# Sixteen sequences through two gated layers on one Trainium2 core: the output gate's products taken out of the first norm's loop, the routing of layer 0 put ahead of the first chunk's gates, and each group's stores issued as two pairs

## The chip, the core and the metric

The kernel runs on one core of a Trainium2 chip. The core has TensorE (PE, matrix products, with its weight loads shown as PEld), VectorE (DVE), ScalarE (ACT), GpSimd (POOL) and SyncE (SP, used here for DMA queues only). The engines run side by side and wait for each other by semaphores. The metric is the device time of one execution in microseconds (us), a median over runs.

## The reference: what is computed

Tokens `x` (16 sequences of 256 tokens of 128 values, 4096 tokens) go through two layers, and each is `x + s * silu(f)`. In layer 0, `s` is a gated linear attention in chunks, and `f` a mixture of 8 experts of which each token uses two; in layer 1, `s` is causal attention with 16 heads and `f` a mixture of 16 experts, again two for each token.

```python
xn = _layernorm(x, axis=-1)
# attention of layer 0: q, k, v, decays gk from a low-rank product, in chunks of 64
gk = jax.nn.log_sigmoid(x @ Wgk1 @ Wgk2 + bgk2) / GATE_NORM
o = _gla_chunk(q, k, v, gk)
g = (x @ Wg).reshape(B, T, H, DV)
o = o * jax.lax.rsqrt(jnp.mean(o * o, axis=-1, keepdims=True) + EPS) * gnw
o = o * (g * jax.nn.sigmoid(g))
s = o.reshape(B, T, H * DV) @ Wo
# experts of layer 0
gate_scores = jax.nn.softmax(jnp.einsum('btd,ed->bte', x, Wg), axis=-1)
topk_val, topk_idx = jax.lax.top_k(gate_scores, TOP_K)
...
x = x + s * g
```

`g * sigmoid(g)` of the attention is the output gate that the change moves; its products are `xn @ Wg`.

## The kernel before, in words

All engines follow one walk, a fixed order of steps written in `walk`; each engine's block gives its own body for a step. The order on an engine is therefore the order of the walk, and a wait holds back everything behind it on that engine.

**First norm (0 to about 44 us).** `norm(0, g)` runs over 8 groups of 512 tokens, in stages that lag behind each other: DVE centres and takes variances, ACT scales, PE turns the rows (L385), DVE moves them to `xnT` (L1228), PE makes the routing logits (L368), DVE moves those (L1246) and chooses two experts for each token (`choose`, L1270 to L1286). Behind each group's logits PE makes the output gate's product of that group (L374, 128x512 f32, eight in all) and ACT applies Silu (L831).

**First gates and routing (44 to about 60 us).** `gla(-1)` and `gla(0)` make the low-rank gate product (`gate_in` L419), its rest (`gate_out` L431), the gate logarithms on ACT (`gate_logs` L891 to L895) and the sigmoids on DVE (L1372). Then `route(0)`: PE counts tokens of each expert (L405), ACT moves the counts (L855), and DVE works out the slot of each row of each token (L1304 to L1318), then the experts of each group and the mixing weights (L1323 to L1344).

**Scatter (60 to about 155 us).** POOL writes the 8192 token rows to their slots in HBM (`xs`) with 64 indirect DMAs (L1718), spread over the walk's `gla(1)` to `gla(6)`. Two of a chunk's steps are POOL's too: `chunk_ends` (L1748), which waits for the exponentials of the decays (ACT L904, behind DVE's scan L1380), and `output_gates` (L1754), which waits for `o_rs` of ACT L941. DVE's `set_later` (L1189 to L1201) prepares constants; it stands in the walk behind the first scatter step of `t=1`.

**Experts of layer 0 with the attention (155 to about 414 us).** 18 groups of 512 rows. For group `g`, SP loads its rows, PE turns them (L558), makes the products with the expert's weights in two halves of two experts (`expert_up`, L594 to L598) and, a group later, the product down (L608); DVE adds the bias (L1477); POOL stores four blocks of 128 rows by indirect DMA (`store`, L1734, 4 for a group). Until `t=19` chunk steps of the attention stand between them: on PE `key_values` (L482), `outputs` (L496, L503) and others, on DVE the scan L1380, `states` (L1400 to L1408) and `gated` (L1431). Four PSUM banks go round among all these products, so a product can wait for an older one's bank; the bank of `key_values` is free when DVE L1406 has read it.

**Join, second norm, routing, scatter, experts of layer 1 (414 to 970 us).** The same machinery, with 20 groups and with the attention's heads between them (`mha`). In a group's loop POOL multiplies tanh by sine (`product1`, L1774), copies the slots' ids (L1727), adds phases (L1769) and stores (L1734). Then a last join to the end at 1017.6 us.

## Time and profile before

| | |
|---|---|
| Time, median of 3 runs | 1022.38 us (1019.39 to 1028.81) |
| Time of the profiled execution | 1020.89 us |
| Its span (first to last instruction) | 1017.6 us |
| PE busy | 758.3 us (75%) |
| DVE busy | 641.5 us (63%) |
| ACT busy | 633.3 us (62%) |
| POOL busy | 468.1 us (46%) |

The profile is of one execution. A busy share is an average over stages with different limits, so each stage is read by itself: which engine has no gaps there, and what its first instruction waited for. PE runs at one of two clock levels, 1.2 or 2.4 GHz; the column PEclk is the granted share of full speed.

### The profile page before, as it was taken

Reading aid. Unit: us, or ns where it says so; the run is one execution under the profiler, and the core shown is the slowest. Engines: PE = TensorE matmul, PEld = TensorE weight load, DVE = VectorE, ACT = ScalarE, POOL = GpSimd, SP = SyncE. Lnnn points to the kernel's source line nnn. Section 1 sums busy time; section 2 is a strip of 40 time slices with the busy share of each in tenths; the row PEclk is TensorE's granted clock in tenths of the full one; section 3 lists DMA queues with packets and bytes.
Section 4 is the critical chain, followed back from the end, with each engine's and each line's share of the span. In section 5 each row is a group of like instructions: output and inputs, shape, how many; then the busy total and the mean of one; then the engine's idle time right before and its main releaser. Section 6 shows DMA issues by size and latency. Waiting matters only on the chain.

```text
span 1017.6 us, 23699 instructions
## 1 busy us (share of the span) xinstructions
PE 758.3 (75%) x8916; PEld 600.5 (59%) x8916; DVE 641.5 (63%) x1113; ACT 633.3 (62%) x1151; POOL 468.1 (46%) x477
## 2 busy tenths in 40 slices
PE   4738678999999989057692788678878878878650
PEld 3427567888888988035471455456756756666530
DVE  7587555767676433597767676366467567566537
ACT  5437455777766532257461455566979878888756
POOL 4137882324242355542000777313656556556622
PEclk9659778999999999577796798689999999999985
DMA  9702211011111111700000533200111111111053
GB/s 312 281 23 69 73 58 51 23 33 33 34 30 36 43 54 46 194 11 1 1 2 0 193 94 114 61 12 25 41 33 38 39 33 41 35 34 30 22 154 107
DMA packets 62366, 63.92 MB, mean 63 GB/s; under 512 B 7378, under 2 KB 52322, under 8 KB 62132
## 3 DMA queue, kind: packets, MB, share of 16 engines
q1 hardware_dynamic: 53300, 43.99, 14.9%
q0 software_dynamic: 8960, 18.43, 5.5%
q8 instruction: 77, 1.26, 0.5%
q14 instruction: 29, 0.24, 0.1%
HBM read 31.84 MB, written 30.55 MB: 61 GB/s over the span
## 4 chain that ended last, share of the span: by engine, by line
PE 41%; DVE 20%; POOL 13%; issue 13%; ACT 9%; DMA 2%; SPq 0%; POOLq 0%; DVEq 0%; ACTq 0%
POOL xs L1718 8%; PE bank L594 4%; POOL ys L1734 4%; PE bank L442 3%; PE bank L596 3%; DVE arena L1592 3%; PE bank L657 3%; PE bank L595 2%; PE bank L722 2%; PE bank L608 2%; PE bank L482 2%; PE bank L622 2%; ACT L805 2%; ACT arena L1115 2%; DVE arena L1530 2%
## 5 line engine op out<-in xcount | busy, mean ns | idle before, releaser
L1734 POOL DMA_INDIRECT ys<-arena x152 | 171.6, 1129 | 182.7 <-DVE arena L1477 75.3
L1718 POOL DMA_INDIRECT xs<-arena x128 | 131.6, 1028 | 61.8 <-issue 33.9
L594 PE MATMUL bank<-arena 128*128 128x128 bf16 x608 | 138.9, 235 | 11.7 <-DVE arena L1592 6.5
L596 PE MATMUL bank<-arena 128*128 128x128 bf16 x608 | 138.6, 235 | 0.0
L595 PE MATMUL bank<-arena 128*128 128x128 bf16 x608 | 136.2, 231 | 0.0
L1115 ACT ACTIVATE arena<-bank 128x512 f32<-128x512 f32 x192 | 99.0, 605 | 54.2 <-PE bank L710 54.2
L1592 DVE TENSOR_REDUCE arena<-bank 128x2 bf16<-128x512 f32 (+1 forms) x192 | 118.9, 683 | 14.0 <-PE bank L683 14.0
L805 ACT ACT_TABLE_LOAD x72 | 92.4, 1283 | 1.3
L442 PE MATMUL bank<-arena 128*128 128x256 f32 x256 | 69.3, 431 | 15.4 <-DVE arena L1364 15.4
L594 PEld LDWEIGHTS bank<-arena 128*128 x608 | 63.5, 104 | 28.2 <-issue 18.8
L1505 DVE TENSOR_SCALAR arena<-bank 128x512 f32<-128x512 f32 x40 | 27.6, 691 | 74.5 <-ACT arena L1012 74.5
L1580 DVE SCALAR_TENSOR_TENSOR arena<-arena,bank 128x512 bf16<-128x512 bf16 x64 | 46.0, 745 | 44.2 <-ACT arena L1088 42.9
L442 PEld LDWEIGHTS bank<-arena 128*128 128x128 f32 x256 | 54.7, 220 | 25.2 <-DVE arena L1364 16.1
L1774 POOL TENSOR_TENSOR arena<-arena 128x1024 f32<-128x1024 f32 x19 | 44.6, 2348 | 49.5 <-ACT arena L1026 49.4
L596 PEld LDWEIGHTS bank<-arena 128*128 x608 | 62.6, 103 | 5.4 <-issue 1.0
L598 PE MATMUL bank<-arena 128*128 x288 | 64.5, 224 | 0.1
L657 PE MATMUL bank<-arena 128*128 128x256 f32 x256 | 63.6, 393 | 0.7 <-issue 0.7
L595 PEld LDWEIGHTS bank<-arena 128*128 x608 | 63.7, 105 | 0.2
L1467 DVE SCALAR_TENSOR_TENSOR arena<-arena,bank 128x512 f32<-128x512 f32 x36 | 24.6, 689 | 44.7 <-ACT arena L988 44.7
L657 PEld LDWEIGHTS bank<-arena 128*128 128x128 f32 x256 | 47.6, 196 | 8.3 <-issue 2.5
L988 ACT ACTIVATE arena<-bank 128x512 f32<-128x512 f32 x36 | 21.5, 598 | 45.7 <-PE bank L598 45.6
L1680 POOL TENSOR_TENSOR arena<-arena 128x4 f32<-128x4 f32 x16 | 16.2, 1013 | 72.5 <-DVE arena L1211 72.5
(214 smaller groups left out, 1971.6 us busy)
## 6 DMA issues: line engine op xcount, KB each, us to landing
xs<-arena SPq DMA_DIRECT2D x19, 516.0 KB, 8.1
arena<-xs SPq DMA_DIRECT2D x38, 258.0 KB, 2.8
arena<-ys SPq DMA_DIRECT2D x32, 256.0 KB, 5.3
arena<-in_MF SPq DMA_DIRECT2D x8, 512.0 KB, 4.2
ys<-arena POOLq DMA_INDIRECT x152, 2.3
arena<-in_x SPq DMA_DIRECT2D x8, 256.0 KB, 5.5
arena<-in_W SPq DMA_DIRECT2D x8, 256.0 KB
xs<-arena POOLq DMA_INDIRECT x128, 2.4
```

What stands on the lines that cost most here:

```text
L442: i = mm(k[:, 256 * h:256 * h + 256], (Wq, Wk)[n // 2][:, 128 * hh:128 * hh + 128], xnT[:, cols])
L594: mm(o, hi, b[:, 0, c4], stop=False)
L595: mm(o, hi, b[:, 1, c4], start=False, stop=False)
L596: i = mm(o, lo, b[:, 0, c4], start=False, stop=(l == 1))
L598: i = mm(o, b1r[:, 128 * c:128 * c + 128], b1s[:, bass.DynSlice(v * 128, 128)], start=False)
L657: j = mm(k[:, 256 * z:256 * z + 256], Wqk[:, c:c + 128], xnT[:, 256 * b:256 * b + 256])
L805: eng.preload_act_table_set(name)
L1115: act(PT[kt_][:, i, gs[0]:gs[0] + len(gs), :], bank_of["s2", b, n, i][:, :].rearrange("p (g q) -> p g q", q=w), ACT.Exp, scale=8 ** -0.5). ...
L1580: stt(T, hiT[n % 2], low_of[n // 2], bank_of["qk1", b, n][:, :], ALU.mult, ALU.add).then_inc(m_qk_moved.sem, 1)
L1592: red(negM[b % 2][:, u, 32 * i + gs[0]:32 * i + gs[0] + len(gs)], kv_, op=ALU.max, negate=True).then_inc(m_max.sem, 1)
L1718: eng.indirect_dma_start(xs[l][:, :], bass.IndirectOffsetOnAxis(ap=slot_i[l][:, m:m + 1], axis=0), xrow[:, t, :], None).then_inc(rows_move ...
L1734: eng.indirect_dma_start(ys[l][:, :], bass.IndirectOffsetOnAxis(ap=yid[g % 4][:, j:j + 1], axis=0), y[:, 128 * j:128 * j + 128], None).the ...
```

## The change

The walk's step `route` is cut in two, `route` and `route_end`; the products of the output gate become a step `silus` of their own; `store` takes a pair of blocks at a time.

```diff
             for g in range(NG + 5):
                 do["norm"](0, g)
                 if g == 4:
                     do["set_gates"]()
-            for t in range(-1, 1):
-                for part in range(3):
-                    do["gla"](t, part)
+            for part in range(3):
+                do["gla"](-1, part)
+            do["silus"](0, 2)
             do["route"](0)
+            do["silus"](2, NG)
+            for part in range(3):
+                do["gla"](0, part)
             for t in range(1, 7):
                 for part in range(3):
                     do["scatter"](0, 3 * (t - 1) + part, 18)
...
                 for c in range(8 * (t - 1) // 6, 8 * t // 6):
                     do["w1"](c)
+                if t == 1:
+                    do["route_end"](0)
...
             do["route"](1)
+            do["route_end"](1)
...
-                    if l == 0:
-                        b = bank(("silu", h), silu_done.at(h))
-                        if h == 0:
-                            eng.wait_ge(*ld["wvg"].at(0))
-                        mm(b[:, :], Wvg[:, 128:256], xnT[:, 512 * h:512 * h + 512]).then_inc(silu.sem, 1)
+
+            def silus(a, e):
+                for h in range(a, e):
+                    b = bank(("silu", h), silu_done.at(h))
+                    if h == 0:
+                        eng.wait_ge(*ld["wvg"].at(0))
+                    mm(b[:, :], Wvg[:, 128:256], xnT[:, 512 * h:512 * h + 512]).then_inc(silu.sem, 1)
...
-                h = due(l, CHOOSE, g)
-                if h is not None and l == 0:
-                    table(TANH_SIN)
+
+            def silus(a, e):
+                table(TANH_SIN)
+                for h in range(a, e):
                     eng.wait_ge(*silu.at(h))
                     act(s_all[:, 4 * h:4 * h + 4, :].rearrange("p t d -> p (t d)"), bank_of["silu", h][:, :], ACT.Silu).then_inc(silu_done.sem, 1)
...
+            def route_end(l):
                 if l == 0:
                     spread(0)
                     spread(1)
...
                 step(red(R["sl"], inc.rearrange("p (e b) -> p b e", e=E), op=ALU.add), 13)
                 step(cp(slot_i[l], R["sl"]), 14)
-                ef = R["ef"]
+
+            def route_end(l):
+                E, R, C = EXPERTS[l], RS[l], routed[l]
+                cu, en, ef, step = R["cu"], R["en"], R["ef"], step_of(C)
...
-            def store(l, g):
+            def store(l, g, pair):
                 y = (yb0, yb1)[l][g % 2]
-                eng.wait_ge(*y_out[l].at(g))
-                eng.wait_ge(*ids_moved[l].at(g))
-                for j in range(4):
+                if pair == 0:
+                    eng.wait_ge(*y_out[l].at(g))
+                    eng.wait_ge(*ids_moved[l].at(g))
+                for j in (2 * pair, 2 * pair + 1):
...
             def experts0(g, part):
+                if part == 0 and g >= 2:
+                    t = OUTPUTS_EARLY + g
+                    eng.wait_ge(*(kv.at(t - 3) if t < 19 else up[0].at(g, 1) if g < 18 else down[0].at(17)))
+                    store(0, g - 2, 1)
                 if part == 0 and g + 1 < GROUPS[0]:
                     ids(0, g + 1)
                 if part == 2 and g >= 1:
-                    store(0, g - 1)
+                    store(0, g - 1, 0)
+                    if g == 18:
+                        store(0, 17, 1)
...
             def experts1(g, part):
+                if part == 0 and 2 <= g < 20:
+                    eng.wait_ge(*up[1].at(g, 1))
+                    store(1, g - 2, 1)
                 if part == 0 and 1 <= g < 20:
                     product1(g - 1)
...
                 if part == 2 and g >= 1:
-                    store(1, g - 1)
+                    store(1, g - 1, 0)
+                    if g >= 19:
+                        store(1, g - 1, 1)
```

Below, PE's order from the end of the norm's loop to the second chunk's gates. L385 turns rows, L368 makes logits, L374 the output gate's product, L419 and L431 the chunk gates (`gate_in`, `gate_out`), L405 the counts. Before:

```order
L385 MATMUL bank<-arena 128x128 x4
L368 MATMUL bank<-arena 128x8 x4
L374 MATMUL bank<-arena 128x512
L368 MATMUL bank<-arena 128x8 x4
L374 MATMUL bank<-arena 128x512
L419 MATMUL bank<-arena 80x256
L431 MATMUL bank<-arena 128x256 x4
L419 MATMUL bank<-arena 80x256
L405 MATMUL bank<-arena 128x256 x4
L431 MATMUL bank<-arena 128x256 x4
```

The same place after the change, where line numbers are those of the changed file (L393 turns rows, L374 makes logits, L382 the output gate's product, L429 and L441 the chunk gates, L413 the counts):

```order
L393 MATMUL bank<-arena 128x128 x4
L374 MATMUL bank<-arena 128x8 x8
L429 MATMUL bank<-arena 80x256
L382 MATMUL bank<-arena 128x512 x2
L413 MATMUL bank<-arena 128x256 x4
L382 MATMUL bank<-arena 128x512 x6
L441 MATMUL bank<-arena 128x256 x4
L429 MATMUL bank<-arena 80x256
L441 MATMUL bank<-arena 128x256 x4
```

The counts now come ahead of the first `gate_out`, and six of the eight products of the output gate stand between the counts and it.

DVE's order behind the cast of the slots (L1335 in the changed file). L1384 and L1392 are the chunk gates, L1202 to L1214 are `set_later`, L1400 is the scan, L1441 and L1443 scale queries and keys, L1373 a part of the expert weights, and L1343 opens `route_end`, of which three rows are shown:

```order
L1335 CAST arena<-arena 128x64 [waits routed0]
L1384 TENSOR_TENSOR arena<-bank,arena 16x256 [waits gate1_hi,routed0]
L1392 SCALAR_TENSOR_TENSOR arena<-bank,arena 128x512 [waits gate2_ln]
L1392 SCALAR_TENSOR_TENSOR arena<-bank,arena 128x512
L1202 CAST arena<-arena 128x128 x3
...
L1400 SCALAR_TENSOR_TENSOR arena<-arena 128x1024 [waits decay,set_pool]
...
L1373 TENSOR_TENSOR arena<-arena 128x512 [waits w1_hi]
L1343 TENSOR_TENSOR arena<-arena 128x320
...
L1357 TENSOR_REDUCE arena<-arena 128x32 [waits chosen_exp,routed_exp,routed0]
...
L1364 TENSOR_TENSOR arena<-arena 128x32 [waits routed0]
L1400 SCALAR_TENSOR_TENSOR arena<-arena 128x1024 [waits decay,routed0]
```

Before, the two sigmoid rows stood ahead of the whole routing, and all of the routing ahead of `set_later` and the first scan; now the rest of the routing stands between the first and the second scan.

POOL's order in a loop of the experts of layer 0, before (L1754 `output_gates`, L1727 ids, L1748 `chunk_ends`, L1734 stores):

```order
L1754 TENSOR_TENSOR arena<-arena 128x256 [waits o_rs]
L1727 COPY arena<-arena 128x4 [waits ld_rows0,stored_y0]
L1748 COPY arena<-arena 128x12 [waits state,exp_decay]
L1734 DMA ys<-arena 9216x128 [waits ids_moved0,y_out0]
L1734 DMA ys<-arena 9216x128 x3
```

and after the change (L1781, L1747, L1775 and L1755 in the same roles):

```order
L1781 TENSOR_TENSOR arena<-arena 128x256 [waits o_rs]
L1755 DMA ys<-arena 9216x128 [waits kv]
L1755 DMA ys<-arena 9216x128
L1747 COPY arena<-arena 128x4 [waits ld_rows0,stored_y0]
L1775 COPY arena<-arena 128x12 [waits state,exp_decay]
L1755 DMA ys<-arena 9216x128 [waits ids_moved0,y_out0]
L1755 DMA ys<-arena 9216x128
```

Two of the four stores that stood ahead of the next loop's `output_gates` now stand behind it.

## Rows read from the trace of the kernel before

**Rows 1.** POOL's timeline, the scatter: start, duration, what, [idle before, releaser]

```profile
59.91 1.28 POOL L1718 DMA_INDIRECT xs<-arena  x1 [12.43 <-DVE arena L1318]
...
67.93 0.95 POOL L1718 DMA_INDIRECT xs<-arena  x1 [0.30 <-issue]
72.66 0.20 POOL L1748 COPY arena<-arena 128x12 f32<-128x12 f32 x1 [3.77 <-ACT arena L904]
...
86.23 0.20 POOL L1748 COPY arena<-arena 128x12 f32<-128x12 f32 x1
...
154.25 0.97 POOL L1718 DMA_INDIRECT xs<-arena  x1 [0.30 <-issue]
```

**Rows 2.** Windows, experts and attention of layer 0: stretch, length, busy of each engine

```profile
180.00:344.00 164.00, 160.99 (x2192) 143.08 (x2193) 112.17 (x186) 117.66 (x190) 57.60 (x65) 1.00 0.12 33
```

**Rows 3.** PE's timeline, products of the output gate (L374) and logits

```profile
24.46 1.10 PE L374 MATMUL bank<-arena 128*128 128x512 f32 x2
...
38.27 2.06 PE L374 MATMUL bank<-arena 128*128 128x512 f32 x2
40.12 1.71 PE L368 MATMUL bank<-arena 128*128 128x8 f32 x8
```

**Rows 4.** DVE's timeline from the last logits to the second scan

```profile
41.87 0.19 DVE L1246 COPY arena<-bank 128x32 f32<-128x32 f32 x1 [3.22 <-PE bank L368]
...
46.74 0.42 DVE L1364 TENSOR_TENSOR arena<-bank,arena 16x256 bf16<-16x256 f32 x1
...
53.09 1.22 DVE L1304 TENSOR_TENSOR_SCAN arena<-arena 128x512 f32<-128x512 f32 x1
...
59.41 0.20 DVE L1318 CAST arena<-arena 128x64 int32<-128x64 f32 x1
...
64.98 0.50 DVE L1189 CAST arena<-arena 128x128 bf16<-128x128 f32 x3
...
69.22 2.28 DVE L1380 TENSOR_TENSOR_SCAN arena<-arena 128x1024 f32<-128x1024 bf16 x1
...
79.33 2.33 DVE L1380 TENSOR_TENSOR_SCAN arena<-arena 128x1024 f32<-128x1024 bf16 x1
```

**Rows 5.** ACT's timeline, the table load, the gate logarithms and the counts

```profile
45.02 1.28 ACT L805 ACT_TABLE_LOAD   x1
47.87 1.09 ACT L891 ACTIVATE arena<-bank 128x512 f32<-128x512 f32 x2 [1.56 <-PE bank L431]
...
51.30 1.43 ACT L855 ACTIVATE arena<-bank 128x256 f32<-128x256 f32 x4
```

**Rows 6.** Windows of 2 us: PEclk stands behind the busy times

```profile
58.00:60.00 2.00, 0.96 (x3) 0.23 (x1) 1.90 (x4) 0.00 (x0) 0.09 (x1) 0.73 0.00 0
```

**Rows 7.** Timeline of all engines, a loop in the middle of layer 0's experts

```profile
249.84 2.27 POOL L1734 DMA_INDIRECT ys<-arena  x1 [0.30 <-issue]
...
252.12 0.91 DVE L1404 TENSOR_TENSOR arena<-arena 128x128 f32<-128x128 f32 x1
252.14 0.73 POOL L1754 TENSOR_TENSOR arena<-arena 128x256 f32<-128x256 f32 x1
```

**Rows 8.** Waits by releaser, 165 to 344 us: sum in us, times, longest

```profile
PE bank L594 <- DVE arena L1406: 2.8, 7, 0.4
```

**Rows 9.** Timeline of all engines, the loop before any store is due

```profile
181.93 0.29 DVE L1404 TENSOR_TENSOR arena<-arena 128x128 f32<-128x128 f32 x1
```

**Rows 10.** Timeline of all engines, the last chunk step beside the experts

```profile
362.88 0.73 POOL L1754 TENSOR_TENSOR arena<-arena 128x256 f32<-128x256 f32 x1
...
364.78 1.38 PE L608 MATMUL bank<-arena 128*128 128x128 f32 x10 [2.75 <-DVE arena L1467]
```

**Rows 11.** Timeline of all engines, a loop of layer 1's experts

```profile
899.90 2.34 POOL L1774 TENSOR_TENSOR arena<-arena 128x1024 f32<-128x1024 f32 x1 [4.74 <-ACT arena L1026]
...
902.34 2.03 POOL L1769 TENSOR_TENSOR arena<-arena 128x512 f32<-128x512 f32 x2
...
904.77 1.23 DVE L1492 SCALAR_TENSOR_TENSOR arena<-arena 128x1024 f32<-128x1024 f32 x1 [0.27 <-ACT arena L1020]
```

More of the change, by code:

```diff
@@ L793, in nothing @@
                 pass
-            walk({"setup": nothing, "set_gates": nothing, "set_later": nothing, "norm": norm, "norm_end": norm_end, "gla": gla, "route": route, "scatter": nothing, "w1": nothing,
+            walk({"setup": nothing, "set_gates": nothing, "set_later": nothing, "norm": norm, "norm_end": norm_end, "gla": gla, "route": route, "route_end": route_end, "silus": silus, "scatter": nothing, "w1": nothing,
                   "ffn0_begin": lambda: turn(0, 0), "ffn0": ffn0, "mha_begin": all_banks, "join": nothing, "last_join": nothing, "mha1": mha1, "mha2": mha2,
@@ L1163, in nothing @@
                 pass
-            walk({"setup": nothing, "set_gates": nothing, "set_later": nothing, "norm": norm, "norm_end": norm_end, "gla": gla, "route": route, "scatter": nothing, "w1": w1,
+            walk({"setup": nothing, "set_gates": nothing, "set_later": nothing, "norm": norm, "norm_end": norm_end, "gla": gla, "route": route, "route_end": route_end, "silus": silus, "scatter": nothing, "w1": w1,
                   "ffn0_begin": lambda: hi(0, 0), "ffn0": ffn0, "mha_begin": nothing, "join": join, "last_join": last_join, "mha1": mha1, "mha2": mha2,
@@ L1288, in choose, with step_of, step @@
                         eng.wait_ge(*C.at(h, s - 1))
+            def step_of(C):
+                def step(i, k):
+                    i.then_inc(C.sem, 1)
+                    eng.wait_ge(*C.at(0, k))
+                return step
             def route(l):
                 E, R, C = EXPERTS[l], RS[l], routed[l]
-                N, sh2 = 64 * E, [128, E, 64]
+                N, sh2, step = 64 * E, [128, E, 64], step_of(C)
                 O = one_hot[:, 0:N]
@@ L1296, in route @@
                 first = inc3[:, :, 0:1].rearrange("p e o -> p (e o)")
-                def step(i, k):
-                    i.then_inc(C.sem, 1)
-                    eng.wait_ge(*C.at(0, k))
                 eng.wait_ge(*counts.at(l))
@@ L1318, in route, with route_end @@
                 step(cp(slot_i[l], R["sl"]), 14)
-                ef = R["ef"]
+            def route_end(l):
+                E, R, C = EXPERTS[l], RS[l], routed[l]
+                cu, en, ef, step = R["cu"], R["en"], R["ef"], step_of(C)
                 for i in range(2):
@@ L1635, in nothing @@
                 pass
-            walk({"setup": setup, "set_gates": set_gates, "set_later": set_later, "norm": norm, "norm_end": norm_end, "gla": gla, "route": route, "scatter": nothing, "w1": w1,
+            walk({"setup": setup, "set_gates": set_gates, "set_later": set_later, "norm": norm, "norm_end": norm_end, "gla": gla, "route": route, "route_end": route_end, "silus": nothing, "scatter": nothing, "w1": w1,
                   "ffn0_begin": lambda: lo(0, 0), "ffn0": ffn0, "mha_begin": mha_begin, "join": join, "last_join": last_join, "mha1": mha1, "mha2": mha2,
@@ L1805, in nothing @@
                 pass
-            walk({"setup": setup, "set_gates": nothing, "set_later": nothing, "norm": norm, "norm_end": nothing, "gla": gla, "route": route, "scatter": scatter, "w1": nothing,
+            walk({"setup": setup, "set_gates": nothing, "set_later": nothing, "norm": norm, "norm_end": nothing, "gla": gla, "route": route, "route_end": nothing, "silus": nothing, "scatter": scatter, "w1": nothing,
                   "ffn0_begin": begin0, "ffn0": experts0, "mha_begin": nothing, "join": join, "last_join": last_join, "mha1": nothing, "mha2": nothing,
@@ L1910, in nothing @@
                 pass
-            walk({"setup": setup, "set_gates": nothing, "set_later": nothing, "norm": nothing, "norm_end": nothing, "gla": nothing, "route": route, "scatter": nothing, "w1": nothing,
+            walk({"setup": setup, "set_gates": nothing, "set_later": nothing, "norm": nothing, "norm_end": nothing, "gla": nothing, "route": route, "route_end": nothing, "silus": nothing, "scatter": nothing, "w1": nothing,
                   "ffn0_begin": lambda: begin(0), "ffn0": experts0, "mha_begin": mha_begin, "join": join, "last_join": last_join, "mha1": nothing,
```

## The prediction, made before the changed kernel ran

> **What bounds the kernel now.** I read the timelines of the first 100 us engine by engine, then the windows by stage, then the waits and the chain of waits of each stage.
>
> The first stage that matters is the scatter. POOL's first store to `xs` starts at 59.91, the last of 64 at 154.25, at a pitch of about 1.26, and POOL stands still only once: its seventh store starts at 67.93 and the next thing is `chunk_ends` at 72.66, after 3.77 us of waiting for ACT's exponentials. The second `chunk_ends`, at 86.23, waits for nothing [rows 1]. So POOL sets the end of this stage, and what counts is when it starts and how long it is held at `chunk_ends`. Layer 0's experts begin right behind the last store.
>
> From 180 to 344 us PE is busy for 160.99 of 164 us [rows 2]; only its small gaps can be won there. The waits name one kind: seven times 0.4 us, sum 2.8, in which PE's L594 waits for DVE L1406 to free a bank [rows 8].
>
> **Part 1: the routing earlier.** The sum is made against the profiled execution: span 1017.6, time 1020.89, which is 1.5 under the median of 1022.38.
>
> The last logits are moved at 41.87 [rows 4]. Ahead of them PE has two output gate products; one takes 1.85 from start to start at the low clock (38.27 to 40.12) [rows 3]. Taking them away can give between 0 and 3.7. ACT's last scaling of the rows comes at its own time, so I take 2.5: logits at 39.4. Choosing takes 4.9 (41.87 to 46.74) and ends at 44.3. Before, the routing's scan came at 53.09 [rows 4], because `gate_out`, the logarithms and the sigmoids stood ahead. Now only the counts on PE and their copies on ACT (1.43 [rows 5]) do, some 2.1 together. The two output gate products ahead of them (3.7) fit beside the choosing. The scan comes at about 46.4, 6.7 earlier. The slots follow 6.3 behind it as before (53.09 to 59.41), so POOL starts at 53.2 and has its seven stores out at 62.2 in place of 68.9.
>
> Then it waits for `chunk_ends(0)`, and here the moved work is late. Six output gate products stand on PE ahead of `gate_out(0)`. PE can begin them at 45.4, when the first count is copied. At the low clock they take 6 x 1.85 = 11.1 and end at 56.5. At the high clock the row is 1.10 in place of 2.06 [rows 3], so about 6 x 0.99 = 5.9, ending at 51.3. Which it is the clock decides. PE is dense here from 39.4 on, apart from the counts; before, PE was dense from 52.7 on and the clock rose shortly before 60 (mean 0.73 in that window) [rows 6]. I let it rise midway: the products end at E = 53, bounds 51.3 and 56.5.
>
> Behind E come the last Silu (0.6), ACT's table load (1.28), which was hidden so far and now is not, the logarithms and the gate's move (47.87 to 51.30, 3.4) [rows 5], and DVE's gate and sigmoids (1.7, the time from there to 53.09). That is E + 7.0. `set_later` is now ahead of the scan and behind the sigmoids, 4.24 (64.98 to 69.22) [rows 4]. The scan starts at E + 11.3 = 64.3 in place of 69.22: 4.9 earlier, between 6.6 and 1.4. POOL gets `chunk_ends(0)` as much earlier, at 67.8, having stood for 5.6.
>
> Next, `route_end` (5.3, between the cast at 59.41 + 0.20 and 64.98) now stands between the first and the second scan. Before, the second scan (79.33, 2.33 long [rows 4]) and ACT's exponential of 1.1 behind it made `chunk_ends(1)` possible at 82.8, and POOL came at 86.23 [rows 1]: a slack of 3.4. Set back by 5.3 it is late by 1.9, once; the third scan has more slack. ACT's chain of the third chunk waits with it, but is not waited for.
>
> Part 1 gives 4.9 - 1.9 = **3.0**, bounds 4.7 and -0.5. All stages behind shift with it.
>
> **Part 2: the stores in pairs, layer 0.** In seven loops the fourth store of a group falls under DVE's scan and takes 2.27 in place of 0.96. `output_gates` comes right behind it at 252.14, together with DVE's L1404 at 252.12, which takes 0.91 [rows 7] against 0.29 in the loop before any store is due [rows 9]. The 0.6 pass on to L1406 and cost PE the 0.4. With only two stores ahead, `output_gates` runs under the scan as in that earlier loop, and L1404 is free. I take all 7 x 0.4 = **2.8**, bounds 0 and 3.5 (half a microsecond a loop, if PE's pace behind the gap gains too).
>
> A rule speaks against it. The Trainium skill, "SBUF — State Buffer", section "Who interferes with whom", says that a VectorE instruction with two SBUF inputs contends with a GpSimd instruction that reads SBUF, and that whichever starts first blocks the other wholly. The second pair now comes just as L1404 does. By the rule a store of 0.96 could hold L1404 as long as `output_gates` does now, and this term would be 0; the 0.91 of rows 7 agrees with the rule.
>
> At 362.88 `output_gates` of the last chunk comes behind four stores; DVE and with it PE's L608 wait, PE for 2.75 [rows 10]. With two stores of 1.27 fewer ahead it comes 2.5 earlier. PE saves **2.5**, bounds 0 and 2.75. In the loops without attention the two pairs follow each other without a gap, since the products up (under 2 us after the product down) are done before the first pair is out: 0. The ids and the row loads have more than a loop of slack: 0.
>
> **Part 2, layer 1.** The second pair now stands ahead of `product1` and waits for the second product up; the sine comes about 2.1 behind the same event, the pair takes 2.5. So `product1` (899.90) is late by some 0.3. The phases behind it end at 904.37, and DVE's L1492 starts at 904.77, released by ACT [rows 11]: 0.4 of slack hold the 0.3. Value 0, bounds 0 and a loss (below).
>
> **Sum.** 3.0 + 2.8 + 2.5 = 8.3. Span 1009.3, time 1012.6; from the median instead, 1014.1. I forecast 1013.5.
>
> **The rivals.**
>
> *The clock stays low over the six products.* For it: before, PE was at the low clock from 36 to 58 with dense stretches in it. Against: those stretches held logits of 8 columns between the big products, and the new one does not. Then part 1 gives -0.5 and the time is about 1017.
>
> *The collision moves.* POOL's second pair takes the place of `output_gates` beside L1404, and the 2.8 are lost: about 1016. For it: the pair is released at just that place. Against: a store is longer by the scan, not the scan by a store. This is also what the skill's rule named above would do.
>
> *Slower: `product1` late in layer 1.* If DVE stretches the second pair (as the 2.27 above), `product1` is late by 1.3 more. From 0.4 on it decides: what goes beyond is paid in each of some 16 loops. At 1.6 late it is 1.2 x 16 = 19 us lost, less 8.3 won: about 1033. Against: only PSUM readers run on DVE in that stretch.
>
> *All at their better bounds.* 4.7 + 3.5 + 2.75 = 11: about 1011.
>
> *The change does nothing.* POOL's wait at `chunk_ends(0)` takes up the whole lead and PE's gaps in layer 0 stay: 1021 to 1022.
>
> **How the numbers follow.** Chances: forecast 0.46, low clock 0.17, collision moves 0.13, all at the better bounds 0.16, nothing 0.05, slower 0.03. About 1% (10 us) is what a measurement of this kernel can tell from no change: faster is below 1012.2, slower above 1032.6. Faster: the better bounds, and a third of the forecast's case, since 1013.5 is near the line: 0.31. Slower 0.03. Within 1%: 0.66. The forecast's own range is 1010 to 1017; the one that holds 8 in 10 reaches to the low clock and the moved collision, 1007 to 1020, as the three runs of before alone lie up to 6 us from their median.
>
> **What would show it.** Right: the first store to `xs` near 53; a wait of 4 to 7 us ahead of the first `chunk_ends` and about 2 ahead of the second; the last store to `xs` near 151; L1404's successor at 0.29 in the loops and no 0.4 in front of the first product up's second half; no 2.75 ahead of L608. Wrong: the six products at 1.85 each; `chunk_ends` holding POOL again for the third chunk; VectorE's wrap in layer 1 released by POOL's phases in more than the three loops in which it is now. A first store later than 56 would mean that I misread what the counts wait for.

## The result, and the profile after

| | before | after |
|---|---|---|
| Time, median | 1025.45 us (12 runs, 1019.17 to 1032.25) | 1015.97 us (12 runs, 1010.69 to 1019.68) |
| Time of the profiled execution | 1020.89 us | 1015.84 us |
| Its span | 1017.6 us | 1014.0 us |

The ratio of the times is 0.9892, with a 95% interval of 0.9869 to 0.9916: about 1.1% or 11 us faster, and the interval does not reach 1. The two profiled executions differ by only 3.6 us of span; where the rest is, is a question of its own below.

POOL's timeline of the scatter (start, duration, what, idle before and who ended it), which answers to [rows 1]. L1738 is the store to `xs`, L1775 `chunk_ends`:

```profile
53.83 1.19 POOL L1738 DMA_INDIRECT xs<-arena  x1 [7.86 <-DVE arena L1335]
...
61.83 0.96 POOL L1738 DMA_INDIRECT xs<-arena  x1 [0.30 <-issue]
66.55 0.20 POOL L1775 COPY arena<-arena 128x12 f32<-128x12 f32 x1 [3.77 <-ACT arena L917]
...
82.25 0.20 POOL L1775 COPY arena<-arena 128x12 f32<-128x12 f32 x1 [2.82 <-ACT arena L917]
...
149.83 0.96 POOL L1738 DMA_INDIRECT xs<-arena  x1 [0.31 <-issue]
```

The first store is 6.1 us earlier than before and so is the first `chunk_ends`. The second has a wait that was not there and is 4.0 earlier; the last store is 4.4 earlier.

DVE's timeline, as [rows 4]: last logits (L1259), the slots' scan (L1321), their cast (L1335), `set_later` (L1202) and the first two decay scans (L1400):

```profile
40.34 0.19 DVE L1259 COPY arena<-bank 128x32 f32<-128x32 f32 x1 [1.51 <-PE bank L374]
...
47.00 1.23 DVE L1321 TENSOR_TENSOR_SCAN arena<-arena 128x512 f32<-128x512 f32 x1 [1.35 <-ACT arena L866]
...
53.33 0.20 DVE L1335 CAST arena<-arena 128x64 int32<-128x64 f32 x1
...
58.84 0.53 DVE L1202 CAST arena<-arena 128x128 bf16<-128x128 f32 x3
...
63.12 2.28 DVE L1400 TENSOR_TENSOR_SCAN arena<-arena 128x1024 f32<-128x1024 bf16 x1
...
78.80 2.29 DVE L1400 TENSOR_TENSOR_SCAN arena<-arena 128x1024 f32<-128x1024 bf16 x1
```

PE's timeline from the last turned rows (L393) and logits (L374) to the six products (L382, as [rows 3]):

```profile
36.00 1.09 PE L393 MATMUL bank<-arena 128*128 128x128 f32 x4
36.88 3.42 PE L374 MATMUL bank<-arena 128*128 128x8 f32 x16
...
41.06 3.62 PE L382 MATMUL bank<-arena 128*128 128x512 f32 x4
...
46.19 5.42 PE L382 MATMUL bank<-arena 128*128 128x512 f32 x12
```

The last six products take 5.42 us, 0.9 each: the high clock. The two ahead of them, from 41.06, take 3.62, or 1.81 each: the low one. The trace's record of the clock begins only at 45.5 us, with the rise to the high level, and a window ahead of the first entry is printed as 1.00. The durations tell what the clock was there. Four turned rows take 1.09 at 36.00; in the kernel before the same instructions (L385) take 0.60 in a stretch whose record says 1.00, and 1.06 in one whose record says 0.50:

```profile
30.41 0.60 PE L385 MATMUL bank<-arena 128*128 128x128 f32 x4
...
35.85 1.06 PE L385 MATMUL bank<-arena 128*128 128x128 f32 x4
```

So TensorE is at the low clock until 45.5 in after, where in before it rises first at 21.5 and falls at 35.2. In after it falls at 55.8, while PE is empty (from 52.5 to 58.5).

A loop in the middle of layer 0's experts, DVE and POOL, as [rows 7, 9] (L1781 `output_gates`, L1755 stores, L1424 the old L1404):

```profile
240.84 2.28 DVE L1400 TENSOR_TENSOR_SCAN arena<-arena 128x1024 f32<-128x1024 bf16 x1
...
243.91 0.29 DVE L1424 TENSOR_TENSOR arena<-arena 128x128 f32<-128x128 f32 x1
```

```profile
242.12 1.52 POOL L1781 TENSOR_TENSOR arena<-arena 128x256 f32<-128x256 f32 x1 [2.13 <-ACT arena L954]
243.79 1.01 POOL L1755 DMA_INDIRECT ys<-arena  x1 [0.15 <-issue]
245.10 0.96 POOL L1755 DMA_INDIRECT ys<-arena  x1 [0.30 <-issue]
```

The waits by releaser no longer have a row in which PE waits for this line's successor [rows 8]. At the last chunk step PE's product down follows without the 2.75 us of [rows 10], and from 180 to 344 us PE is busy for 163.67 of 164 us, where [rows 2] had 160.99 (the changed kernel is some 7 to 10 us further on in the walk there):

```profile
352.22 2.05 PE L618 MATMUL bank<-arena 128*128 128x128 f32 x16
```

```profile
180.00:344.00 164.00, 163.67 (x2234) 146.18 (x2210) 107.28 (x187) 117.00 (x190) 56.65 (x69) 1.00 0.12 34
```

### The profile page after: what moved, and what is told of

Same layout as the page of the kernel before. It is cut to its first block, busy times and chain, and to the rows that moved or that the text cites. A ratio compares the mean times of both kernels' runs of the same rounds, so it can differ in the third digit from the quotient of the medians.

```text
span 1014.0 us, 23701 instructions
## 1 busy us (share of the span) xinstructions
PE 776.7 (77%) x8916; PEld 611.3 (60%) x8916; DVE 637.6 (63%) x1113; ACT 634.5 (63%) x1151; POOL 460.2 (45%) x477
## 4 chain that ended last, share of the span: by engine, by line
PE 49%; DVE 19%; ACT 13%; issue 10%; POOL 5%; DMA 2%; SPq 1%; DVEq 0%; ACTq 0%; POOLq 0%
PE bank L452 6%; PE bank L604 4%; PE bank L667 4%; DVE arena L1612 3%; PE bank L606 3%; PE bank L618 3%; PE bank L732 3%; PE bank L605 3%; ACT L815 2%; ACT arena L1128 2%; PE bank L632 2%; POOL ys L1755 2%; PE bank L720 2%; PE bank L374 2%; DVE arena L1550 1%
## 5 line engine op out<-in xcount | busy, mean ns | idle before, releaser
L1755 POOL DMA_INDIRECT ys<-arena x152 | 158.7, 1044 | 215.5 <-ACT arena L1057 72.0
L1738 POOL DMA_INDIRECT xs<-arena x128 | 130.8, 1022 | 57.6 <-issue 34.3
L604 PE MATMUL bank<-arena 128*128 128x128 bf16 x608 | 137.9, 233 | 9.7 <-DVE arena L1612 6.7
L1128 ACT ACTIVATE arena<-bank 128x512 f32<-128x512 f32 x192 | 98.8, 602 | 56.8 <-PE bank L720 56.8
L604 PEld LDWEIGHTS bank<-arena 128*128 x608 | 62.4, 103 | 26.4 <-issue 16.4
L452 PE MATMUL bank<-arena 128*128 128x256 f32 x256 | 70.8, 438 | 4.5 <-DVE arena L1384 4.5
L667 PE MATMUL bank<-arena 128*128 128x256 f32 x256 | 65.7, 403 | 0.7 <-issue 0.7
L606 PEld LDWEIGHTS bank<-arena 128*128 x608 | 61.9, 102 | 5.3 <-issue 0.5
L452 PEld LDWEIGHTS bank<-arena 128*128 128x128 f32 x256 | 55.9, 225 | 14.7 <-DVE arena L1384 4.9
L605 PEld LDWEIGHTS bank<-arena 128*128 x608 | 63.0, 104 | 0.2
L667 PEld LDWEIGHTS bank<-arena 128*128 128x128 f32 x256 | 48.9, 201 | 8.8 <-issue 2.5
L393 PE MATMUL bank<-arena 128*128 128x128 f32 x64 | 15.7, 392 | 46.1 <-ACT arena L827 46.1
```

What stands on the lines that cost most here:

```text
L452: i = mm(k[:, 256 * h:256 * h + 256], (Wq, Wk)[n // 2][:, 128 * hh:128 * hh + 128], xnT[:, cols])
L604: mm(o, hi, b[:, 0, c4], stop=False)
L605: mm(o, hi, b[:, 1, c4], start=False, stop=False)
L606: i = mm(o, lo, b[:, 0, c4], start=False, stop=(l == 1))
L667: j = mm(k[:, 256 * z:256 * z + 256], Wqk[:, c:c + 128], xnT[:, 256 * b:256 * b + 256])
L1128: act(PT[kt_][:, i, gs[0]:gs[0] + len(gs), :], bank_of["s2", b, n, i][:, :].rearrange("p (g q) -> p g q", q=w), ACT.Exp, scale=8 ** -0.5). ...
```

## The experiments

Each kernel was profiled once and timed beside the kernel before on the same chip. The profiled executions are compared by stretches, in us, read from the timelines: the first store to `xs`; from it to the last one; on to the ninth `chunk_ends`; ten chunk steps to the last `chunk_ends`; on to layer 0's last store to `ys`; on to the slots' scan of layer 1's routing; the third loop of layer 1's experts (from one wrap, L1512, to the next); the seventeen after it; the last store to `ys` to the end.

| kernel | 1st `xs` | scatter | to 9th | ten steps | to last `ys` | to routing | loop 3 | 17 loops | end |
|---|---|---|---|---|---|---|---|---|---|
| before | 59.9 | 94.3 | 51.1 | 122.0 | 86.2 | 135.7 | 21.0 | 253.8 | 42.7 |
| before, again | 58.3 | 95.4 | 51.0 | 122.1 | 86.1 | 135.6 | 21.1 | 253.8 | 45.5 |
| part 1 only | 53.6 | 96.7 | 52.6 | 122.2 | 86.2 | 138.5 | 22.9 | 253.5 | 42.6 |
| part 2 only | 60.8 | 94.4 | 50.5 | 119.4 | 83.4 | 137.9 | 24.0 | 254.4 | 42.6 |
| after | 53.8 | 96.0 | 48.2 | 119.5 | 82.4 | 138.8 | 24.1 | 254.9 | 45.5 |
| pairs in layer 0 only | 54.2 | 97.3 | 49.2 | 119.5 | 82.4 | 135.6 | 21.1 | 253.7 | 42.6 |
| `route_end` at t=2 | 55.6 | 95.7 | 48.5 | 119.4 | 82.4 | 135.2 | 21.1 | 254.5 | 42.7 |
| `set_later` later | 54.2 | 97.1 | 49.3 | 119.5 | 82.3 | 138.5 | 24.1 | 254.7 | 42.7 |
| products in the loop | 55.7 | 93.0 | 49.4 | 119.5 | 82.4 | 135.2 | 21.2 | 254.0 | 45.3 |
| `route_end` at t=4 | 53.9 | 95.0 | 50.7 | 119.5 | 82.4 | 135.7 | 21.1 | 254.3 | 42.7 |

Part 1 only, after and pairs in layer 0 only run the same instructions up to the last store to `xs`. Their scatters of 96.0 to 97.3 us, and last stores at 149.8, 150.3 and 151.4, show how far one profiled execution is from another there; a difference of about 1 us in the first two columns is not read as an effect below.

### Part 1 alone

The change without its pairs:

```diff
-                    store(0, g - 2, 1)
...
-                    store(0, g - 1, 0)
+                    store(0, g - 1, 0)
+                    store(0, g - 1, 1)
```

(and the same in layer 1.)

> The walk of the change (output gate products out of the first norm's loop, layer 0's routing ahead of the first gates, the rest of the routing between the first two scans), with a group's four stores together as before. Theory A, the two parts add: in the profiled executions the changed kernel was 13.6 us ahead when its last layer 0 store landed, of which 2.6 over the seven loops and 2.6 at the last chunk step belong to the pairs. Without them the lead there is about 8.4, PE's seven waits of 0.4 on DVE are back, and the time is about 5.5 us under the kernel before (ratio 0.9946). Theory B, the earlier start is taken up by the clock of later stages, so that the whole gain of the change is the pairs': ratio 0.998 to 1.001.

Measured: ratio 0.9917 (0.9891 to 0.9943), median 1015.63. That is more than A said (its 0.9946 lies just outside), and B is excluded. The collision is back, from DVE's timeline and from the waits between 165 and 346 us:

```profile
249.59 0.91 DVE L1424 TENSOR_TENSOR arena<-arena 128x128 f32<-128x128 f32 x1
```

```profile
PE bank L604 <- DVE arena L1426: 2.8, 7, 0.4
```

The lead at the last layer 0 store was not 8.4 but 2.3 us in the profiled execution, which with 1021.39 us was the longest of its six; of these it lost 1.5 to the first execution of before in the stretch behind the scatter. So one profiled execution does not show what the median does.

### Part 2 alone

```diff
-                for j in range(4):
+                for j in (2 * pair, 2 * pair + 1):
```

with the calls of the change, in the old walk.

> The kernel before with only the stores in pairs, in both layers. Theory A, the terms as forecast: the seven waits of PE on DVE (2.8 us) and the 2.75 us wait of the last chunk step go, 5.3 us in all, ratio 0.9948. Theory B, pairs remove a collision only together with the earlier start: 0.998 to 1.000. Theory C, the pairs of layer 1 cost about 1 us (the lead shrank from 7.4 to 6.3 us over the seventeen later loops of layer 1): ratio 0.9958, with the loops of layer 1 longer than before.

Measured: ratio 0.9945 (0.9917 to 0.9972). A, and C is as near. The stretches say more: ten steps take 119.4 in place of 122.0, the stretch behind them 83.4 in place of 86.2. So 2.5 and 2.7 us, with the old start. In that second stretch one L1404 still takes 0.89 (at 347.89), and the stretch is 1.0 longer than with part 1 as well, where none does. By their ratios the two parts alone are worth 8.5 and 5.6 us, together more than the 11 of the whole; the intervals are wide enough for that, and no more is read from it.

### Pairs in layer 0 only

```diff
-                if part == 0 and 2 <= g < 20:
-                    eng.wait_ge(*up[1].at(g, 1))
-                    store(1, g - 2, 1)
```

> The changed kernel with the stores of layer 1 four together again. Theory A, the pairs of layer 1 are worth nothing: the same time as the changed kernel, ratio 0.989 against the kernel before. Theory B, they cost the 1.1 us of lead that went over seventeen loops: ratio 0.988 and a lead that does not shrink in those loops. Theory C, they are worth something: above 0.990.

Measured: ratio 0.9912 (0.9878 to 0.9946), which does not tell the theories apart. The seventeen loops do, a little: 253.5 to 253.8 us in the four executions without pairs in layer 1, 254.0 to 254.9 in the six with them. The pairs cost there 0.8 on the mean. Part of it is the clock: in part 2 only, after and `set_later` later it is low for 19 us in these loops, in the others for 11 to 12. The three kernels with pairs and the shorter low clock take 0.6 more than the four without pairs. One place where that is seen is loop 15 to 16 of the kernel with `route_end` at t=4, 15.35 us against 14.96 here:

```profile
893.35 1.23 DVE L1512 SCALAR_TENSOR_TENSOR arena<-arena 128x1024 f32<-128x1024 f32 x1 [0.69 <-POOL arena L1796]
```

DVE's wrap waits for POOL's phases (L1796), which stand behind the late `product1`. The other place is the last wrap, which POOL releases in all six kernels with pairs in layer 1 and ACT (after 2.77, in this kernel) in those without; that loop is 0.1 us longer:

```profile
954.26 1.22 DVE L1512 SCALAR_TENSOR_TENSOR arena<-arena 128x1024 f32<-128x1024 f32 x1 [2.88 <-POOL arena L1796]
```

That is B, a little smaller than it said, and on two loops' evidence.

### The kernel before, once more

> The kernel before once more, for a second profiled execution. Theory A, what the changed kernel lost between the two layers (3.1 us), in the third loop of layer 1 (3.0 us) and in the last join (2.7 us) is TensorE's granted clock, which falls in other places from one execution to the next: the same stages of this execution differ from the first of the same kernel by one to three us in the places where the granted clock differs, and by under 0.3 us elsewhere. Theory B, these losses come from the change: this execution's stages are as long as the first one's within 0.3 us.

Measured: span 1020.1. The first store is 1.6 us earlier and the scatter 1.1 longer than in the first execution; six of the other seven stretches agree within 0.2 us, but the last one is 45.5 in place of 42.7: the same kernel, 2.8 us longer, where the changed kernel "lost" 2.8. The other two losses of the changed kernel, 3.1 us up to the routing and 3.0 in loop 3, are absent in four kernels that run the same instructions there (pairs in layer 0 only, products in the loop, `route_end` at t=2 and at t=4) and present in part 2 alone, `set_later` later and, in part, part 1 alone. In loop 3 the clock shows it. Windows of 8 us at the same place, of after and then of the kernel with pairs in layer 0 only (PEclk is the third number from the end, as in [rows 6]):

```profile
674.00:682.00 8.00, 8.00 (x63) 6.73 (x64) 4.42 (x6) 3.31 (x7) 0.85 (x1) 0.60 0.00 1
```

```profile
673.50:681.50 8.00, 8.00 (x126) 6.42 (x130) 5.90 (x8) 5.26 (x11) 3.05 (x3) 1.00 0.06 19
```

Both are busy throughout; one has 0.60 of the clock and does half as many products. No second pair has been issued by then (POOL's first store of layer 1 comes behind it), so this is no work of the change. Theory A for loop 3 and the end. For the stretch up to the routing the clock also differs: its mean over the stretch is 0.71 in after and 0.76 in both executions of before, and the four longest of these stretches in the table are the four with the most low clock. But the two executions of before are alike there, and why it was low for longer only in changed kernels is open.

### The rest of the routing, a chunk later

```diff
-                if t == 1:
+                if t == 2:
                     do["route_end"](0)
```

> The changed kernel with the rest of the routing (route_end) a chunk later, between the second and the third scan. Theory A, POOL's 2.82 us in front of the second chunk_ends are DVE's 5.4 us of route_end ahead of the second scan: that wait goes, the third chunk_ends (exponential done at 95.5, POOL there at 94.9) waits 0.6 instead, and the last store to xs comes 2.2 us earlier behind the first one (93.8 in place of 96.0 us). Time 2 us under the changed kernel. Theory B, the second wait is ACT's own chain (logarithms of the next chunk, which stood behind the routing's exponential), and stays.

Measured: ratio 0.9882 (0.9846 to 0.9918). The second `chunk_ends` comes at 81.72 without a wait, so the wait's cause was `route_end`.

But the scatter takes 95.7 in place of 96.0, not 93.8. (The first store, at 55.6, is late because the whole first norm is: PE's first instruction comes at 14.38, against 12.16 in after.) POOL, ahead now, meets the chunk pipeline: `output_gates` at 139.30 waits 1.39 for ACT and is 2.56 long, where after has 1.88 and no such wait.

```profile
139.30 2.56 POOL L1781 TENSOR_TENSOR arena<-arena 128x256 f32<-128x256 f32 x1 [1.39 <-ACT arena L954]
```

### `set_later` behind the first scan

```diff
-                    if t == 1 and part == 0:
-                        do["set_later"]()
...
                 if t == 1:
+                    do["set_later"]()
                     do["route_end"](0)
```

> The changed kernel with set_later (4.3 us of DVE) behind the first scan, in front of route_end. Theory A, DVE's order from the gates to the second scan is one sum, which this edit leaves as it is: the first scan comes 4.3 us earlier and the first chunk_ends waits for nothing (3.77 before), the second one waits 6.6 in place of 2.8 us, and the last store to xs stays where it is against the first (96.0 us). Theory B, what counts is the first wait: 3.8 us earlier.

Measured: ratio 0.9934 (0.9908 to 0.9960). First scan at 59.31, no wait at the first `chunk_ends`, 4.08 at the second (at 82.74), scatter 97.1. A in its effect: the first wait alone is worth nothing, since DVE's sum up to the second scan decides. The second wait is 4.08 and not 6.6, as POOL comes later than A had it: a store now lies under the scan (the fifth takes 2.85). The scatter is 1.1 us longer than in after, which is inside the spread of the three executions of that walk.

### The products back in the loop

```diff
-            do["silus"](0, 2)
             do["route"](0)
-            do["silus"](2, NG)
...
                     expert_logits(l, g)
+                    h = due(l, LOGITS, g)
+                    if h is not None:
+                        silus(h, h + 1)
```

and the same in ACT's `norm`.

> The changed kernel with all eight output gate products and Silus back in the first norm's loop, a group's behind its logits. Theory A (the forecast's step): the last logits come 1.5 to 2.5 us later, the first store to xs at 55.5 in place of 53.8; but no product stands in front of the gates, so the first scan comes at 61.5 in place of 63.1, the first chunk_ends waits under 1 us, and the last store to xs is 1.5 us earlier than in the changed kernel, at 148.3. Theory B, without the products side by side TensorE stays at 1.2 GHz from 36 to 58 us, the counts and the gates come late, and the last store to xs is at 151 to 152.

Measured: ratio 0.9918 (0.9890 to 0.9946). From the timelines: last logits 42.28 (after 40.34), first store 55.65, first scan 61.37, no wait at the first `chunk_ends`, 0.39 at the second, last store at 148.7, which is 1.1 us earlier than in after and 1.6 and 2.7 earlier than in the two other executions with the products taken out. A. PE's clock is low for much of the stretch (mean 0.59 from 36 to 54 us), as B said, but the last store is not late for it. At the last logits the changed kernel is no better off: it too is at the low clock until 45.5, and a group's logits take 1.71 in both. At the high clock they take 0.95, as in the second execution of the kernel before, where the record has 1.00 from 38.1 to 44.9:

```profile
39.31 0.95 PE L368 MATMUL bank<-arena 128*128 128x8 f32 x8
```

That execution moved its last logits at 40.31, with all products in the loop; after has 40.34 without them. In the four executions with the products in the loop the last logits are moved at 40.3 to 43.0, in the six without at 40.1 to 42.1, 1.1 earlier on the mean. So no gain of the products' move is shown beyond that spread, and at the gates it loses. What made part 1 gain is the order of routing and gates and the splitting of the routing: with them alone the last store is still 5.1 to 5.6 us ahead of before.

### `route_end` behind the fourth chunk

```diff
-                    if t == 1 and part == 0:
+                    if t == 2 and part == 2:
                         do["set_later"]()
...
-                if t == 1:
+                if t == 4:
                     do["route_end"](0)
```

> The changed kernel with set_later in the second chunk's steps and route_end behind the fourth chunk's, where DVE is ahead of POOL by more than they take. Theory A, POOL is the bound of this stage and its two waits (3.77 and 2.82) are DVE's order alone: both go, nothing takes their place, and the last store to xs comes 6.6 us earlier behind the first one (89.4 in place of 96.0 us); time 6.6 us under the changed kernel, ratio 0.983 to the kernel before. Theory B, the wait moves to a later chunk_ends or to the experts' beginning, which needs the table of experts: under 3 us gained.

Measured: ratio 0.9893 (0.9843 to 0.9942). Both waits are gone (`chunk_ends` at 64.60 and 78.62), but the scatter takes 95.0, not 89.4. B, in its kind: of 6.6 us one is left at the end (2.2 against the longest of the three like executions). `output_gates` now waits 1.88 at 136.92, and behind the third `chunk_ends` the stage takes 54.6 us in place of 52.1. So POOL was not the bound of this stage any more; that the chunk pipeline of PE, DVE and ACT is right behind it is read from that one wait and the one with `route_end` at t=2.

### Four kernels with a halting TensorE

The last four ran on two chips (one of them that of the four above) on which TensorE halted between products for no reason that the profile shows: the medians of before were 1104 and 1095 us there. The waits of the combined kernel below have such a row, and no kernel above has one like it:

```profile
PE bank L480 <- issue: 11.1, 14, 1.9
```

The first halts stand at 89 to 99 us, so only what lies ahead of them is comparable, and the ratios on the same chip with caution.

The six products behind the first chunk's gates:

```diff
             do["route"](0)
-            do["silus"](2, NG)
             for part in range(3):
                 do["gla"](0, part)
+            do["silus"](2, NG)
```

> The changed kernel with the six later output gate products and their Silus behind the first chunk's gates instead of in front of them (the first two stay beside the choosing). Theory A, the six products are what the first chunk_ends waits for: the first scan comes some 3.9 us earlier (59.2), the first chunk_ends waits for nothing (3.77 before), the second at most 0.5 (2.82 before), the first store to xs stays near 53.8, and the last store comes 93.9 us behind it (96.0 in the changed kernel), at 147.7. Theory B, the products then stand in front of the second chunk's gates with two more table loads of ACT, and that chunk is late by what the first one wins: the second chunk_ends waits 5 us or more and the last store stays at 149.8.

Ratio 0.9818 (0.9747 to 0.9888). First scan 59.78, first `chunk_ends` at 65.03 after 0.94, the second at 80.75 after 2.82 still. Half of A: the six products are what the first `chunk_ends` waits for (3.77 in after), but the second one's wait is that of `route_end` and stays.

The same with the edit of "Pairs in layer 0 only":

> The same, with the stores of layer 1 four together again. Theory A: in layer 1 the seventeen loops from the third on take 253.7 us as in the three executions without pairs there (254.0 to 254.9 in the six with them), the scatter is as in the kernel with the products behind the gates, and the time is the lowest so far, 2 to 3 us under the changed kernel, ratio 0.987. Theory B: the pairs of layer 1 make no difference, 254.3 us in those loops.

Ratio 0.9859 (0.9782 to 0.9936); its loops of layer 1 cannot be compared. Inconclusive.

Three stores and one, with four together in layer 1:

```diff
-                for j in (2 * pair, 2 * pair + 1):
+                for j in ((0, 1, 2), (3,))[pair] if l == 0 else (2 * pair, 2 * pair + 1):
```

> The changed kernel with three stores of a layer 0 group where the first pair stood and one where the second did, and four together in layer 1. Theory A, the loss of the old order is the fourth store alone, which fell under DVE's scan and took output_gates with it: the third store is out 0.8 us ahead of output_gates' event, so output_gates runs under the scan as with pairs, L1424 takes 0.29, PE's seven waits of 0.4 stay away, and the ten loops between the ninth and the last chunk_ends take 119.5 us. Theory B, any store in front of output_gates beyond the second delays it: L1424 at 0.91 in some loops, 121 to 122 us.

Ratio 0.9899 (0.9826 to 0.9972). The ten steps take 119.5 us, L1424 takes 0.29:

```profile
267.64 1.52 POOL L1781 TENSOR_TENSOR arena<-arena 128x256 f32<-128x256 f32 x1 [0.86 <-ACT arena L954]
...
269.42 0.29 DVE L1424 TENSOR_TENSOR arena<-arena 128x128 f32<-128x128 f32 x1
```

A: it was the fourth store alone (all fifteen L1424 take 0.29 to 0.30).

The edits of "The rest of the routing, a chunk later", of the products behind the gates and of "Pairs in layer 0 only" together:

> Three edits on the changed kernel: the six output gate products behind the first chunk's gates, route_end a chunk later, the stores of layer 1 four together. Theory A, the two waits in front of chunk_ends have causes of their own and these edits take one each: 0.9 us left in front of the first (as with the products behind the gates), none in front of the second (as with route_end later), so the last store to xs comes 92 to 93 us behind the first one in place of 96.0, near 146.5; the loops of layer 1 take 253.7 us; the time is 3.5 us under the changed kernel, ratio 0.986 to the kernel before. Theory B, POOL then meets more of DVE's scans and the later chunks' output_gates wait for ACT, as with route_end behind the fourth chunk: 95 us or more between the first and the last store, ratio 0.989.

Ratio 0.9879 (0.9837 to 0.9922). 1.90 us of wait at the first `chunk_ends`, none at the second; from the first store to the third `chunk_ends` 41.3 us against 43.9 in after, though the first halts (from 89.0) already lie in it. Beyond that the halts hide the answer. No kernel here is shown to beat the changed one: the intervals of all but part 2 alone overlap its own, and the lowest ratio, 0.9818, comes from a halting chip, with an interval three times as wide (0.0141 against 0.0047).

## Why the prediction was right, step by step

The forecast was 1013.5 and a range of 1007 to 1020; 1015.97 was measured. Against the 12 runs of before it is 9.5 to 11 us, where the sum said 8.3. The direction, the places and most sizes came out. That the total came so near is in part luck: the sum had no term for what the clock did behind the scatter, and against the two profiled executions of before some of its terms are measured no better than to a microsecond or two.

- **Logits.** Forecast 39.4, measured 40.34: 1.5 won against the first execution of before, not 2.5, and nothing against the second (40.31). What the sum left out is that TensorE stays at the low clock through the whole norm once the products are gone. At the high clock the last two groups' logits would take 1.9 in place of 3.42 (an estimate, from the 0.95 of one group above), and the logits would be moved at 38.8.
- **First store.** Forecast 53.2, measured 53.83, which is 4.5 to 6.1 earlier than in the two executions of before.
- **The six products.** Forecast E = 53 with bounds 51.3 and 56.5; they ended at 51.6, at the high clock. The premise of the rival, a low clock at 45, was true, and so was the forecast's, that the clock rises in this dense stretch; it rose at 45.5, ahead of the first of the six and not halfway through them. In all seven profiled executions with six products at this place the rise comes ahead of them (42.9 to 46.8) and they take 5.42.
- **First scan and first `chunk_ends`.** Forecast 64.3 and 67.8 after a wait of 5.6; measured 63.12 and 66.55 after 3.77. The scan is 1.2 earlier than forecast because E is 1.4 earlier. The wait is shorter by another 0.6, since the first store was that much later than forecast.
- **`route_end` at the second.** Forecast 1.9 late; 2.82 of wait. The experiment with `route_end` at t=2 shows its cause, and the one at t=4 that taking both waits away is worth 1 to 2 us in the end.
- **Part 1.** Forecast 3.0 (bounds 4.7 and -0.5); 4.4 at the last store, 3.9 against the second execution of before, and 2.3 to 4.4 over the three executions of this walk.
- **L1404.** Forecast 2.8; ten steps are 2.5 us shorter in all seven profiled executions with pairs that can be compared. The rival "the collision moves" fell: the store of 243.79 does not hold L1424 at 243.91, the row has 0.29, and no run here shows that a store blocks VectorE. The prediction had stretched the rule to a store. The Trainium skill, "SBUF — State Buffer", section "Who interferes with whom", has it for a GpSimd instruction that reads SBUF, and infers that a `tensor_tensor` and the making of a DMA's descriptors do not meet; the 0.29 agrees with that. The other way round, a long scan against `output_gates`, the trace agrees that they contend: `output_gates`, with inputs in SBUF, takes 1.52 under the scan and 0.73 without it. Which of the two has to start first is not settled: in before L1404 starts at 252.12 and `output_gates` at 252.14, and it is L1404 that is long.
- **Last chunk step.** Forecast 2.5; the stretch is 2.7 to 3.8 shorter. In both executions of before, and in part 1 only, the clock fell behind that wait (the sixteen products took 2.45, after 2.05), and in no kernel with pairs; so the wait cost more than itself.
- **Layer 1.** Forecast 0; the loops cost 0.6 to 0.8. `product1` was late by the 0.3 that I had, but 0.4 of slack does not hold it in every loop. Here the prediction's own sign of being wrong came up: POOL's phases release the wrap in four loops of after (five with the products in the loop or with `route_end` at t=4), where before has three.
- **What no step had.** The stretch from the last store to the ninth `chunk_ends` is 2.9 us shorter in after. The pairs account for some 0.6 of it, as part 2 only shows (50.5 against 51.0 and 51.1 in before). The rest goes with the clock, which falls once more there in before, for 6.8 us, and not in after. The table orders itself by it: no such fall, 48.2 and 48.5; 3.4 us, 49.2 to 49.4; 6.8 us, 50.5 to 51.1; 10.2 us (part 1 only), 52.6. That the change keeps the clock up there is not shown: like kernels differ. The windows of before and of after:

```profile
155.00:170.00 15.00, 11.27 (x97) 10.65 (x96) 8.12 (x14) 7.88 (x12) 4.34 (x6) 0.77 0.22 59
```

```profile
155.00:170.00 15.00, 14.32 (x206) 12.41 (x207) 9.57 (x18) 12.69 (x21) 2.92 (x4) 1.00 0.17 47
```

So in the profiled executions after led by 13.6 us at the last layer 0 store and gave back 3.1, 3.0, 1.1 and 2.8. Of these the 1.1 is the pairs' in layer 1 (in part), the 3.0 and 2.8 are the clock's chance, and the 3.1 is the clock's too but of open cause. The three other kernels with part 1 and layer 0's pairs and without these episodes, and the one that has only that at the end (products in the loop), spanned 1005.9 to 1006.8 us. A profile pair can thus hide two thirds of a gain of 1%. Open remains why part 1 alone measures 8.5 us (5.9 to 11.2) by its ratio, when its own steps give 2.3 to 4.4; the clock behind the scatter gave some 2 us more in after, but took 1.5 in the profile of part 1 alone.

## What to carry to other kernels

Removing a wait at one place of an in-order chain is worth what the next one leaves: of two waits with 6.6 us, taken away together, one to two microseconds reached the end of the stage, because another chain was close behind. When a short instruction suddenly takes three times its time, look at what was pushed beside it: a single store under a scan delayed POOL's multiplication onto it and cost TensorE 0.4 us in each loop, and moving that one store was enough. Before a gain of 1% is read from two profiles, take a second profile of the kernel before and compare stage by stage. And before a clock of 1.00 is believed, look at how long a known instruction takes there: a window without a clock record is printed as 1.00.

## What was not expected of the hardware

- Taking work out of the first norm kept the clock low. In the four profiled executions with the products in the norm's loop (before twice, part 2 only, products in the loop) the clock first rises at 21.0 to 25.9 us and falls at 34.7 to 36.1; in the ten without them it first rises at 42.9 to 46.8 and falls at 54.0 to 57.9. Up to the rise four turned rows take 1.06 to 1.12 us, where they take 0.60 at the high clock.
- Logits of 8 columns gain from the high clock like the larger products: 0.95 us a group in place of 1.71.
- Between executions of the same instructions, TensorE can have a further low stretch of 7 us, with PE busy throughout (8.00 of 8 us at a mean clock of 0.60, against 1.00 elsewhere); such an episode costs about 3 us.
- At times TensorE halts for about 1 us between products with nothing awaited; the kernel before then takes 1095 to 1104 us (medians), and one chip showed both behaviours.
